# A Fourier-layer chain on one Trainium2 core: the low-mode product in whole chunks, its result turned by TensorE, part of the symmetrising moved to GpSimd

## The reference, cut to what matters

```
x = x + conv3x3(gn(x)) + b
x = x + recurrent_scan_over_columns(gn(x))
x = x + irfft2( W2[:, :, :16, :16] * rfft2(gn(x))[:, :, :16, :16] )     # low modes only
x = x + irfft2( W3 * rfft2(gn(x)) ) + bias
# gn: mean and variance of each image over 2 channels x 64 x 64, eps 1e-5
# both products: out[b,o,k,l] = sum_i x_hat[b,i,k,l] * W[i,o,k,l], complex
```

## Time and profile before

| | us |
|---|---|
| median of 3 runs | 582.54 (581.66 to 582.75) |
| the profiled execution | 583.71 |
| its span | 581.9 |
| PE busy | 531.0 (91%) |
| DVE busy | 473.1 (81%) |
| ACT busy | 392.7 (67%) |
| POOL busy | 298.0 (51%) |
| mean granted TensorE clock | 0.992 |

### The profile page before, as it was taken

One profiled execution on the slowest core, in us unless ns is written; L12 is line 12 of the kernel. 1 busy time (PEld: TensorE's weight loads), 2 busy tenths in 40 slices (PEclk: granted clock), 3 DMA queues, 4 the chain that ended last, 5 costly groups with the idle time before them and its releaser, 6 DMA issues.

```text
span 581.9 us, 28732 instructions
## 1 busy us (share of the span) xinstructions
PE 531.0 (91%) x11428; PEld 419.8 (72%) x11428; DVE 473.1 (81%) x1270; ACT 392.7 (67%) x832; POOL 298.0 (51%) x424
## 2 busy tenths in 40 slices
PE   3999999699999999999999999998878997999995
PEld 2333333477777777777777899997667986899995
DVE  7678885569898989898989778879976898477876
ACT  2445979867777777777777968765748997566441
POOL 7565664046666666666666322005658889320100
PEclk9999999979999999999999999999999999999999
DMA  6910000011111111111111400000307887203325
GB/s 212 397 21 0 2 2 5 1 43 44 38 44 37 45 36 45 36 45 36 45 36 37 146 3 2 0 1 3 110 17 236 268 277 225 67 1 147 145 107 184
DMA packets 26043, 45.80 MB, mean 79 GB/s; under 512 B 5632, under 2 KB 16128, under 8 KB 25104
## 3 DMA queue, kind: packets, MB, share of 16 engines
q1 hardware_dynamic: 24912, 44.98, 24.4%
q10 hardware_dynamic: 672, 0.15, 0.1%
q0 software_dynamic: 416, 0.07, 0.1%
HBM read 28.53 MB, written 8.39 MB: 63 GB/s over the span
## 4 chain that ended last, share of the span: by engine, by line
PE 40%; DVE 33%; issue 11%; ACT 8%; POOL 3%; DVEq 2%; DMA 2%; SPq 0%; POOLq 0%; ACTq 0%
PE psum L654 14%; PE psum L683 8%; DVE spec L1364 7%; DVE spec L1356 5%; PE psum L858 5%; DVE spec L1367 5%; PE psum L815 4%; DVE small L1249 3%; PE psum L934 3%; PE psum L782 2%; POOL work L377 2%; ACT work L300 2%; ACT work L377 2%; PE psum L718 2%; DVE spec L1359 2%
## 5 line engine op out<-in xcount | busy, mean ns | idle before, releaser
L718 PE MATMUL psum<-spec,matrices 128*32 128x128 f32 x3024 | 110.0, 279 | 14.1 <-ACT spec L1051 7.3
L718 PEld LDWEIGHTS psum<-spec,matrices 128*32 128x32 f32 x3024 | 76.7, 110 | 45.9 <-ACT spec L1051 45.8
L725 PE MATMUL psum<-spec,matrices 128*32 128x128 f32 x3024 | 107.8, 275 | 0.9 <-DMA spec<-work 0.9
L566 POOL TENSOR_TENSOR spec<-spec 64x128 f32<-64x128 f32 x126 | 70.6, 561 | 72.3 <-DVE spec L1367 72.3
L725 PEld LDWEIGHTS psum<-spec,matrices 128*32 128x32 f32 x3024 | 85.8, 111 | 4.1 <-issue 3.5
L683 PE MATMUL psum<-spec,matrices 128*64 128x512 f32 x384 | 87.2, 611 | 1.0 <-ACT spec L985 1.0
L858 PE MATMUL psum<-work 128*32 128x128 f32 x2368 | 70.1, 274 | 9.8 <-POOL work L377 4.1
L858 PEld LDWEIGHTS psum<-work 128*32 128x32 f32 x2368 | 63.4, 110 | 16.4 <-issue 15.0
L544 POOL TENSOR_SCALAR spec<-image,small 32x960 f32<-32x960 f32 (+1 forms) x48 | 55.5, 1157 | 35.2 <-PE psum L683 22.7
L560 POOL TENSOR_TENSOR image<-image,spec 128x128 f32 (+1 forms) x128 | 69.3, 542 | 0.0
L683 PEld LDWEIGHTS psum<-spec,matrices 128*64 128x64 f32 x384 | 27.3, 140 | 54.3 <-issue 51.3
(11 more groups left out here) (152 smaller groups left out, 854.2 us busy)
## 6 DMA issues: line engine op xcount, KB each, us to landing
work<-w_dram SPq DMA_DIRECT2D x66, 256.0 KB, 3.5
spec<-work SPq DMA_DIRECT2D x124, 64.0 KB, 1.9
image<-x_dram SPq DMA_DIRECT2D x3, 2048.0 KB, 11.8
out_dram<-image SPq DMA_DIRECT2D x3, 2048.0 KB, 7.0
image<-x_dram SPq DMA_DIRECT2D x4, 512.0 KB, 6.0
work<-w_dram SPq DMA_DIRECT2D x1, 2048.0 KB, 7.8
out_dram<-image SPq DMA_DIRECT2D x4, 512.0 KB, 2.9
kept<-const_dram SPq DMA_DIRECT2D x1, 192.0 KB, 5.1
```

Source lines behind the costliest of these rows:

```text
L566: nc.gpsimd.tensor_tensor(straddled(h, ROWS_01, 0), *of, ALU.subtract).then_inc(lower_ready[h], 1)
L718: last = mm(psum[QUARTERS[hm], 4 * h + g, 0:HB], sv[:, g, QUARTERS[hm]], moving[hm], start=starts, stop=True)
L725: last = mm(psum[q, 4 * h + g, 0:HB], sv[:, 3 + g, q], e, start=True, stop=stops)
```

## The change

Small product. VectorE scales a whole chunk into a contiguous buffer as in the large product, `spread` copies it (two quarters by ScalarE, two by GpSimd). ScalarE copies the result bank to SBUF, and TensorE turns it with 16 or 17 matmuls by slices of the identity into a bank of the spectrum's own layout (column 0 with weight one half), so that one addition of 512 columns adds it to the chunk. The squares go: the variance is taken from the old one, plus the gain (2 x + y) y = (x + y)^2 - x^2 of each chunk, formed by VectorE and summed by TensorE. The mirrored part of column 0 is added by four operations behind the first scaling of the large product. Two of three keep-warm runs here go.

Forward loop. The batch statistics of the last group are taken in the loop (two ahead of it, ten per pass instead of eight), `mean_of_all` before the last group, the group sum and variance at the head of its last transform. Spectrum columns 5 and 7 (VectorE), 6 and 8 (ScalarE) of the last group are moved between the first scalings and spreads.

Large product. VectorE keeps the five symmetrising instructions for images 0 to 7 of the real part, GpSimd the five of the imaginary part; all ten for images 8 to 15 go on GpSimd behind its last spread.

The diff, cut to its core:

```diff
@@ GpSimd
-            pool.wait_ge(w_done, 6 * NG)
+            pool.wait_ge(const_in, 32)
+            nc.gpsimd.memset(no_ident, 0.0).then_inc(l2_consts, 1)
+            nc.gpsimd.tensor_scalar(half_ident, cm["ident"][:, 0:C], 0.5, None, ALU.mult).then_inc(l2_consts, 1)
             for i in range(2):
+                pool.wait_ge(*((w_done, 6 * NG) if i else (t_done, 8 * NG)))
                 nc.gpsimd.memset(diag[i], 0.0).then_inc(diag_zeroed, 1)
             for c in range(4):
+                pool.wait_ge(l2_scaled_ready, 2 * c + 2)
                 if c >= 2:
                     pool.wait_ge(l2_done, c - 1)
-                positive(nc.gpsimd.tensor_tensor, c % 2, 3, chunk(c), rstd).then_inc(l2_pool, 1)
-                negated(nc.gpsimd.tensor_tensor, c % 2, 3, chunk(c), neg_rstd).then_inc(l2_pool, 1)
-            for half in range(2):
-                pool.wait_ge(l2_moved, HM * (half + 1))
-                pool.wait_ge(sq_done, 2 * half + 3)
-                for i, (t, m) in enumerate(ON_POOL):
...
-                    add_low(nc.gpsimd.tensor_tensor, t, m, half).then_inc(l2_pool_added, 1)
-            pool.wait_ge(l2_pool_added, HM * 2)
+                for m in (2, 3):
+                    spread(nc.gpsimd.tensor_copy, l2_scaled[c % 2], c % 2, m).then_inc(l2_spread_pool, 1)
+            pool.wait_ge(l2_spread_act, 8)
+            pool.wait_ge(l2_spread_pool, 8)
+            pool.wait_ge(l2_turned, 3)
             nc.gpsimd.memset(diag[2], 0.0).then_inc(diag_zeroed, 1)
...
-                if 20 <= s_ < 30:
+                if 20 <= s_ < 25:
...
+            for k in range(10):
+                pool.wait_ge(sym_pool, 5 + k)
+                symmetrise_step(nc.gpsimd.tensor_tensor, k // 5, 1, t_pool, k % 5).then_inc(sym_pool, 1)
             pool.wait_ge(y_moved, NCHUNK)
-            pool.wait_ge(sym, 10)
-            pool.wait_ge(sym_pool, 10)
+            pool.wait_ge(sym, 5)
+            pool.wait_ge(sym_pool, 15)
@@ TensorE, over_h
+                if last_group:
+                    pe.wait_ge(stat2, B + 2)
+                    mm(psum[:, 7, 0:2 * B], group_m, mv, start=True, stop=True).then_inc(sum2, 1)
...
-                if last_group:
-                    pe.wait_ge(h_act, j * 6 + 2)
-                    pe.wait_ge(stat2, B + 2)
-                    mm(psum[:, 1, 0:2 * B], group_m, mv, start=True, stop=True).then_inc(sum2, 1)
-                pe.wait_ge(h_act, j * 6 + 1)
+                bank = 4 if last_group else 0
+                pe.wait_ge(h_act, j * 6 + (4 if last_group else 1))
@@ TensorE, small product
-            pe.wait_ge(h_act, 6 * NG - 1)
-            keep_warm(WARM_OPERAND, cm["ident"])
+            def turn(c):
+                pe.wait_ge(l2_moved, c + 1)
+                if c >= 2:
+                    pe.wait_ge(l2_added, c - 1)
+                src = l2_result[c % 2].rearrange("p (k r q b) -> p k r q b", k=4, r=2, q=4)
+                dst = psum[:, 4 + 2 * (c % 2), :].rearrange("p (k t r b) -> p k t r b", k=4, t=4, r=2)
+                for t in range(4):
+                    for q in range(4):
+                        o, x_ = dst[C * q:C * q + C, :, t], src[:, :, :, q]
+                        pick, lo = cm["ident"][:, C * t:C * t + C], 0
...
+                        last = mm(o[:, lo:], pick, x_[:, lo:], start=t == 0 and lo == 0, stop=True, skip_group_check=True)
+                last.then_inc(l2_turned, 1)
+            def sum_gain(c):
+                pe.wait_ge(l2_gain_ready, c + 1)
+                if c == 0:
+                    pe.wait_ge(mean_col, 4)
+                mm(psum[:, 7, :], group_m, l2_gain[c], start=c == 0, stop=c == 3).then_inc(gain_summed, 1)
             pe.wait_ge(w2_in, 16)
+            small_product(0)
+            small_product(1)
+            pe.wait_ge(l2_consts, 2)
+            pe.wait_ge(h_act, 6 * NG)
+            pe.wait_ge(h_dve, 3 * NG)
+            turn(0)
+            small_product(2)
+            turn(1)
+            small_product(3)
+            sum_gain(0)
             pe.wait_ge(stat3, 1)
             mm(psum[:, 5, 0:B], group_m, delta, start=True, stop=True).then_inc(sum3, 1)
-            for s_ in range(4, 8):
-                if s_ == 6:
-                    keep_warm(WARM_SQUARES, cm["ident"])
-                sum_squares(s_)
+            turn(2)
+            turn(3)
+            for c in range(1, 4):
+                sum_gain(c)
+            pe.wait_ge(l2_added, 4)
             keep_warm(WARM_NORM, cm["ident"])
+            pe.wait_ge(mirrored, 4)
@@ ScalarE
+                    act.wait_ge(stat2, B + 5)
+                    a(rstd_in[:, 0:B], var[:, 0:B], ACT.Sqrt, bias=eps_c).then_inc(dev2, 1)
-                for n in (0, 1, 2, 4, 6, 8):
+                for n in (0, 1, 2, 4) if last_group else (0, 1, 2, 4, 6, 8):
...
+            act.wait_ge(diag_zeroed, 2)
+            spread_small(0)
+            last_spectrum(6)
+            spread_small(1)
+            last_spectrum(8)
+            move_small(0)
+            spread_small(2)
+            move_small(1)
+            spread_small(3)
+            move_small(2)
+            move_small(3)
@@ VectorE
-                for k in range(8):
-                    v.bn_stats(bn[:, ds(j * 48 + 6 * k, 6)],
+                    for k in range(10):
+                        v.bn_stats(bn[:, ds(j * 60 + (12 + 6 * k), 6)],
...
             with dve.Fori(0, NG - 1) as j:
                 forward(j)
+            mean_of_all()
             forward(NG - 1, True)
+            variance_of_all()
...
+            scale_small(0)
+            last_spectrum(5)
+            scale_small(1)
+            last_spectrum(7)
+            scale_small(2)
+            scale_small(3)
+            v.memset(delta, 0.0).then_inc(mean_col, 1)
+            def gain(c):
+                dve.wait_ge(l2_turned, c + 1)
+                if c:
+                    dve.wait_ge(l2_gain_ready, c)
+                v.scalar_tensor_tensor(out=l2_both, in0=chunk(c), scalar=2.0, in1=turned(c),
+                                       op0=ALU.mult, op1=ALU.add).then_inc(l2_both_ready, 1)
+                dve.wait_ge(l2_both_ready, c + 1)
+                v.tensor_tensor(l2_gain[c], l2_both, turned(c), ALU.mult).then_inc(l2_gain_ready, 1)
+            def add_small(c):
+                v.tensor_tensor(chunk(c), chunk(c), turned(c), ALU.add).then_inc(l2_added, 1)
+            gain(0)
+            add_small(0)
+            mean_column()
+            gain(1)
+            add_small(1)
+            gain(2)
+            gain(3)
+            add_small(2)
...
-            dve.wait_ge(sq_summed, 8)
+            dve.wait_ge(gain_summed, 4)
...
+            add_small(3)
             dve.wait_ge(dev3, 1)
             step3(v.reciprocal(rstd_bank, rstd_in))
...
+            dve.wait_ge(l2_added, 4)
             for s_ in range(STEPS):
                 scale_chunk(s_)
+                if s_ == 0:
+                    mirror(0)
+                    mirror(1)
...
-                if 20 <= s_ < 30:
+                if 20 <= s_ < 25:
                     symmetrise(s_ - 20)
```

More of the change, by code:

```diff
@@ L185, in program @@
         spec9 = conv_m[:, 0:16 * XT]
-        squares = [spare[:, CHUNK * (i + 1):CHUNK * (i + 2)] for i in range(4)] \
-            + [scan_m[:, CHUNK * (i % 2):CHUNK * (i % 2) + CHUNK] for i in range(4)]
-        l2_copy = spare[:, 0:CHUNK]
+        l2_scaled = [work[:, 2 * CHUNK_T * PLANES + i * XS:2 * CHUNK_T * PLANES + (i + 1) * XS] for i in range(2)]
+        l2_result = [work[:, 7680:8192], spare[:, 5 * CHUNK:6 * CHUNK]]
+        l2_gain = [spare[:, CHUNK * i:CHUNK * i + CHUNK] for i in range(4)]
+        l2_both = spare[:, 4 * CHUNK:5 * CHUNK]
+        half_ident, no_ident = sm(C), sm(C)
         nyq = matrices[:, 0:2 * H * B]
@@ L370, in columns_of, with spread @@
             return spec9 if s_ == 4 else chunk(chunk_of(s_))
-        def spread(copy, s_, m, *func):
-            src = scaled[s_ % 4][C * m:C * m + C, :].rearrange("p (n b) -> p n b", b=B)
-            dst = diag[s_ % 3][C * m:C * m + C, :].rearrange("p (n q b) -> p n q b", q=HM, b=B)[:, :, m, :]
+        def spread(copy, src, slot, m, *func):
+            src = src[C * m:C * m + C, :].rearrange("p (n b) -> p n b", b=B)
+            dst = diag[slot][C * m:C * m + C, :].rearrange("p (n q b) -> p n q b", q=HM, b=B)[:, :, m, :]
             return copy(dst, src, *func)
[L379 to L395, removed]
         def symmetrise_step(add, ri, half_b, t_buf, k):
@@ L1456, in _, with scale_small @@
             step2(v.tensor_tensor(dc, dc, shift[0:C, :], ALU.subtract))
-            step2(v.tensor_scalar(neg_rstd, rstd, -1.0, None, ALU.mult))
             settle2()
-            assert n2[0] == B + 10
-            dve.wait_ge(diag_zeroed, 2)
-            for c in range(4):
+            assert n2[0] == B + 8
+            def scale_small(c):
                 if c >= 2:
-                    dve.wait_ge(l2_done, c - 1)
-                for m in range(3):
```

(8 more changed lines are left out.)

195 lines of the change are left out of this document (86 added, 109 removed).

## The result

The changed kernel has a median of 575.68 us (571.37 to 577.36, five executions) against 582.54: ratio 0.9874, 95% interval 0.9837 to 0.9911. The forecast was 572.7 within 569.8 to 576.8: the range held, the likeliest value was 3.0 us too low. The profiled execution, with 571.37, is the fastest of the five; the others have 574.84 to 577.36. That spread of 6 us is the first thing to be explained: the kernel before has 1.1 here (581.66 to 582.75), and 2.0 to 2.8 in the later sets of 9 to 11 executions.

What follows compares the result with a forecast made beforehand. Bound by engine hand-overs in the small stage and GpSimd's spreads late in the large product: -7.2 - 2.8 = -10.0, plus 0.2 for loop branches, -9.8; from 582.54 to 572.7, range 569.8 to 576.8.

Steps and rivals of the forecast that it cites:

- Forward loop: nothing lost: Forward passes: VectorE's idle hides two more batch statistics in the first two; loop branches cost 0 to 0.5, taken as 0.
- The last transform's start: End of third forward pass: late by-w copies delay the last transform to 396.2, costing 1.4 (bounds 1.0 and 2.0).
- The small stage, -7.2 (laid out -7.6): Last transform to first large product: it starts at 425.8 against 433.40; -7.2 taken, bounds -8.5 and -4.
- The large product, -2.8: Last eight steps: without GpSimd's symmetrising they run at TensorE's 1.85 each, saving 2.8; bounds 0 and -3.2.
- my bound of 3.2: Large product: the largest saving allowed from moving GpSimd's symmetrising behind its last spread.
- the pace of 1.89: Large product: time per step over seven steps taken as before the symmetrising; evidence that weight loads might limit.
- the first rival: Large product keeps its length because the weight stream stands behind GpSimd's wait; only -7.0 left, 575.5; chance 0.14.
- GpSimd's tail: Behind GpSimd's last spread: ten symmetrising instructions, about 6.5, until about 504, hidden by an idle of 18.88.
- The clock: Gaps before turn 2 and addition 3: fewer keep-warm matmuls let the clock fall, +7 in all, 590; chance 0.03.
- My sign of being wrong: After 400: a drop of the granted clock there was listed among the signs that the prediction is wrong.
- The sum without the clock: Whole kernel: -9.8 from 583.71 gives 573.9 for the profiled execution.
- Two SBUF inputs: Small product's scales beside GpSimd's spreads: 0.3 possible on scale 1, taken by slack; 1.2 if all four stretch; counted 0.

Runs made afterwards that it cites:

- the undisturbed profile: Changed kernel as first measured against the kernel before, profiled in its fastest execution: 571.37 us at mean granted clock 0.995; median 575.68.
- the second profile: Changed kernel run again unchanged: median 573.78 us, ratio 0.9839; its profiled execution was the slowest, 577.70 at mean granted clock 0.987.
- the experiment with PSUM: Changed kernel with late means and early keep-warm, scales 1 to 3 reading the reciprocal deviation from PSUM instead of SBUF: 570.32 us, ratio 0.9789.

## Why the prediction was right, and where it was off

*Forward loop: nothing lost.* Right: 57.10 against 57.09 over three passes.

*The last transform's start.* I had the transform 1.75 later with the group sum in front of it; it came 10.64 behind the last over-w start instead of 9.28, 1.4 later. VectorE's twelve late copies took 6.81, not 7.2: it caught up more than I took from a pair. The step that failed stands beside this one. I wrote that the lateness costs 1.4 and left out that TensorE's wait grows from 1.64 to 2.7; by my own numbers it would have been 3.1, but I called 1.9 its longest gap.

*The small stage, -7.2 (laid out -7.6).* Right: -7.3 in the undisturbed profile. The gain operations took 0.69 with 0.73 and 0.60 to the next, addition 3 stood beside the Sqrt, the mirror was hidden, and the large product began right behind keep-warm. Its inner order was less exact: TensorE waited 0.90 and 0.44 for GpSimd's stretched spreads, which I had not, and VectorE caught up more at the start.

*The large product, -2.8.* The mechanism was right and the size too small. The eight last steps took 14.5 to 14.9 in every trace with the move, 17.7 in both without. (My own 17.8 less 14.8 is 3.0; I wrote 2.8.) The whole product took 64.2 to 66.4 over the ten profiles with the move and 68.84 and 67.82 without it. That is 2.4 to 4.6 under the kernel before, and in nine of the ten beyond my bound of 3.2. The part beyond the eight steps, up to 1.5, I had put at nothing. It lies in the 25 steps ahead of them, 49.6 to 51.6 with the move and 50.1 and 51.1 without, so it is mostly variation and not shown to come from the move. I also misread the pace of 1.89: the seven steps from 468.04 on were not free of the symmetrising, since GpSimd's first such instruction stands right among them (GpSimd in the kernel before):

```profile
472.00 0.70 POOL L407 TENSOR_TENSOR matrices<-spec 32x248 f32<-32x248 f32 x1
```

So that pace said less for the first rival than I took it to. That rival, that the weight stream takes GpSimd's place, is seen as single waits (0.69 for w_dram at 433) and not as a rate. GpSimd's tail took 6.8 (6.5 forecast) and was hidden.

*The clock.* This is the term that was mis-sized, and, as far as the mean clocks tell, the main reason why the likeliest value is 3 us too low. I gave the fall a chance of 0.03 and a price of 17 us, as if it either stayed away or lasted through the stage. (The three terms of that price add up to 21.6, not 19.) Of the waits I said only that similar ones had left full clock. In the runs it is neither. It falls for a short stretch at one or two places in a part of the executions, at 1.6 to 1.7 us each, 3.3 for both. My sign of being wrong, a granted clock that drops after 400, came true in this way at keep-warm. One of the two places (before addition 3) I had named, the other, before the last transform, I had not. The changed kernel's executions at 0.987 and 0.988 are 3.5 to 6.0 us above the one at 0.995. The falls cover at most 3.3 of that, and the rest is the large product and the scan's start, as far as the second profile tells; the execution with the median time wasn't profiled. The sum without the clock, 573.9 for the profiled execution, stands against 571.37: of the 2.5, 1.4 is upstream of the change, 1.5 the large product, 0.3 the loop and the small stage, and 0.7 goes the other way, behind the last addition to the image. So two errors went opposite ways, the falls left out and the large product put too small, and it is partly luck that the median came to lie only 3.0 off.

*Two SBUF inputs.* The rows with 0.58 and 0.88 gave the right sign. I costed it at 0 in the sum; it is 0.5 of the stage, by the experiment with PSUM. The Trainium skill, GPSIMD Engine Reference, section 1 Specifications, says VectorE instructions with two SBUF inputs contend with GpSimd. By that rule, the experiment agrees: 0.99 and 1.04 with two inputs, 0.69 and 0.41 with one. The change had moved the copy of rstd that VectorE reads in the small product from PSUM to SBUF, and that brought it.

## What to carry to other kernels

When a change lets an engine start later, cost the wait it makes on TensorE as well as the lateness: a wait that grew from 1.64 to 2.7 us cost 1.67 more in some executions, and seven matmuls without a use, or an order that keeps the wait short, took it back in every profile read. If keep-warm matmuls stand ahead of the critical product, let them wait for no more than the buffer that they write. Where one execution is profiled and others are several microseconds off, look at each one's mean granted clock before explaining the median from the profile.

## What was not expected of the hardware

The granted clock fell to half for a stretch just after TensorE resumed from waits of 2.70 and 1.73 us, in some executions and not in others of the same kernel (transform 7.21 or 8.88, keep-warm 3.84 or 5.44). Before the first wait stood 7.64 us of matmuls without a stop, before the second shorter work with a wait of 0.26. A VectorE operation of 256 columns with two SBUF inputs took 1.04 beside GpSimd's copies against 0.42 alone, so it was slowed more than the 512-column one (0.99 against 0.69), and GpSimd's copies went from 1.71 to 2.05 a pair.
